# A fused four-block transformer kernel on one core: FFN weight splits moved to earlier places, and copies of the attention stage exchanged between two engines

## The reference, cut to what matters

```python
x = x + L0_xattn(layernorm(x), ctx, ctx)   # 16 heads, 4 kv heads, rotary, causal softmax, @ w_out.T
x = x + L0_ffn(layernorm(x))               # silu(gate) * up, width 1376, with shared and routed low-rank terms
x = x + L1_xattn(layernorm(x), ctx)        # sim = (x @ kv) @ kv.T, normalised over keys, softmax
x = x + L1_ffn(layernorm(x))               # 64 experts, 8 per token, width 192
```

## Time and profile before

| | |
|---|---|
| median of 3 runs | 1283.7 us (1283.13 to 1284.74) |
| profiled execution: time | 1284.93 us |
| profiled execution: span | 1283.1 us |
| mean granted clock of TensorE | 0.984 |
| PE busy | 1193.3 us (93%) |
| DVE busy | 723.9 us (56%) |
| ACT busy | 527.3 us (41%) |
| POOL busy | 483.4 us (38%) |

### The profile page before, as it was taken

One profiled execution on the slowest core, in us unless ns is written; L12 is line 12 of the kernel. 1 busy time (PEld: TensorE's weight loads), 2 busy tenths in 40 slices (PEclk: granted clock), 3 DMA queues, 4 the chain that ended last, 5 costly groups with the idle time before them and its releaser, 6 DMA issues.

```text
span 1283.1 us, 19538 instructions
## 1 busy us (share of the span) xinstructions
PE 1193.3 (93%) x6575; PEld 863.3 (67%) x6575; DVE 723.9 (56%) x1476; ACT 527.3 (41%) x1194; POOL 483.4 (38%) x541
## 2 busy tenths in 40 slices
PE   4899999999999999999999999999899999999990
PEld 3667777667777766777776687777456666666650
DVE  6966565686687678677868857554722222222220
ACT  4875221776412278542237853222333333333320
POOL 0440233462123446113353602121255555555530
PEclk8999999999999999999999999999999999999995
DMA  8012231002333000313300013632789999999847
GB/s 294 4 61 78 108 108 63 1 1 102 110 125 116 34 1 2 142 68 139 105 32 1 35 69 113 229 148 109 288 270 332 360 360 349 347 358 357 216 57 140
DMA packets 45906, 187.04 MB, mean 146 GB/s; under 512 B 6716, under 2 KB 9788, under 8 KB 31364
## 3 DMA queue, kind: packets, MB, share of 16 engines
q1 hardware_dynamic: 30964, 146.18, 30.2%
q0 software_dynamic: 14864, 39.85, 13.5%
HBM read 155.31 MB, written 34.90 MB: 148 GB/s over the span
## 4 chain that ended last, share of the span: by engine, by line
PE 73%; DVE 13%; ACT 5%; DMA 3%; issue 2%; POOL 2%; DVEq 0%; SPq 0%; POOLq 0%; ACTq 0%
PE PS L2568 14%; PE PS L1986 10%; PE PS L1988 10%; PE PS L1987 10%; PE PS L2584 4%; PE PS L2074 3%; PE PS L2588 3%; ACT P L892 3%; PE PS L2093 3%; DVE NM L1424 3%; PE PS L2558 2%; PE PS L2005 2%; DMA WRAW<-in_ffn 2%; PE PS L2385 1%; PE PS L2384 1%
## 5 line engine op out<-in xcount | busy, mean ns | idle before, releaser
L2568 PE MATMUL PS<-WE,XGT 128*128 128x384 f32 x512 | 192.7, 499 | 1.5 <-issue 1.5
L712 POOL CAST HH<-HID 128x512 fp32r<-128x512 f32 x44 | 37.3, 847 | 330.8 <-DVE HID L1792 330.8
L1019 ACT ACTIVATE WHI<-WRAW 128x1280 fp32r<-128x1280 f32 x44 | 56.0, 1273 | 226.5 <-DMA WRAW<-in_ffn 226.5
L1986 PE MATMUL PS<-XTH,WHI 128*128 128x512 f32 x352 | 141.1, 401 | 3.4 <-DVE WLO L1735 3.4
L1988 PE MATMUL PS<-XTH,WLO 128*128 128x512 f32 x352 | 138.2, 393 | 0.0
L1987 PE MATMUL PS<-XTL,WHI 128*128 128x512 f32 x352 | 137.9, 392 | 0.0
L892 ACT ACTIVATE P<-PS,NM 128x512 f32<-128x512 f32 (+3 forms) x256 | 131.9, 534 | 13.9 <-DVE NM L1424 12.9
L2568 PEld LDWEIGHTS PS<-WE,XGT 128*128 128x128 f32 x512 | 87.1, 190 | 56.7 <-issue 22.5
L1970 DVE COPY HMT<-PS 128x256 f32<-128x256 f32 x64 | 27.2, 425 | 163.8 <-PE PS L2577 159.3
L1424 DVE TENSOR_REDUCE NM<-PS 128x2 f32<-128x1024 f32 (+2 forms) x96 | 98.6, 1041 | 31.4 <-PE PS L1995 31.2
L2074 PE MATMUL PS<-ident,P 128*128 128x128 f32 x640 | 93.9, 278 | 14.8 <-ACT P L892 7.0
(11 more groups left out here) (341 smaller groups left out, 2733.1 us busy)
## 6 DMA issues: line engine op xcount, KB each, us to landing
WE<-in_we SPq DMA_DIRECT2D x64, 1152.0 KB
WRAW<-in_ffn SPq DMA_DIRECT2D x44, 1060.0 KB, 5.0
acc<-HN SPq DMA_DIRECT2D x17, 256.0 KB, 5.1
XIN<-in_x SPq DMA_DIRECT2D x4, 1024.0 KB, 6.4
out<-X SPq DMA_DIRECT2D x4, 1024.0 KB, 5.1
out<-acc POOLq DMA_DIRECT2D x1, 4096.0 KB, 23.0
hx<-HN SPq DMA_DIRECT2D x3, 1152.0 KB, 4.5
CTX<-in_ctx SPq DMA_DIRECT2D x4, 256.0 KB, 2.9
```

What stands on the lines that cost most here:

```text
L1019: act.activation(WHI[slot][:, 0:WD], WRAW[slot][:, 0:WD], ACT.Copy).then_inc(S["wg_hi"], 1)
L1986: pe.matmul(dst, a[0], b_[0], start=first, stop=False, **kw)
L2568: mm = pe.matmul(bank(2 + s % 2, 0, 2 * F1), XGT[s % 2][:, k, :], WE[s][:, k * 2 * F1:(k + 1) * 2 * F1], start=(k == 0), stop=(k == KC - 1))
```

## The change

It has four parts.

- **FFN weights.** The down half of chunk 0 and the gate and up half of chunk 1 are split on ACT between XN and the first XTH copies, and on DVE around the XTL operations; `wg_rest(0)` on DVE goes ahead of the first XTL. DVE's large operation of chunk 1 is cut in two, one part before XTL of row tile 3, one after; only its last operation stays behind LG. In chunk 1, `wg_hi(2)` and `wg_rest(2)` go ahead of SIL(1) and HID(1), and `wd_rest(1)` goes behind HID(1). The five clearing matmuls are taken out; the first product in each bank starts it.
- **Last group.** On DVE, the statistics of row tile 1 (`stats_x3(b, 1)`) go from before the maxima of units 4 and 5 to behind them.
- **Copies.** The copy of P(2, 0), the first of row tile 2, goes from DVE to ACT in group 2. In batch 0, and in group 2 of the others, stack 2 is copied by DVE and stack 3 by ACT, in place of the reverse. In group 1 with a tail, KST is copied before the maximum of unit 5. `exp_y(2)` goes further back on ACT.
- **Batch 0's projection.** Without a tail, row tile 2's products for k = 0 to 2 are made behind the last group's output, not ahead of it.

```diff
@@ turning_order
-            order += [("P", g, 2, 0, 1, "a" if g == G - 1 else "d"), ("P", g, 2, 1, 1, "a")]
+            order += [("P", g, 2, 0, 1, "a" if g > 1 else "d"), ("P", g, 2, 1, 1, "a")]
-                order += [("stack", g + 1, 2, "a"), ("stack", g + 1, 3, "d")]
+                order += [("stack", g + 1, 2, "a" if tail and g < 2 else "d"), ("stack", g + 1, 3, "d" if tail and g < 2 else "a")]
@@ scalar, attention
-                    if g == G - 1:
+                    if g > 1:
                         turned(g, 2, 0)
                     turned(g, 2, 1)
-                    if tail and g == 2:
-                        exp_y(2)
...
-                    if g < G - 1:
+                    if tail and g < 2:
                         stack(g + 1, 2, QST[1])
+                    elif g < G - 1:
+                        stack(g + 1, 3, QST[2])
                     if tail and g == 1:
                         exp_y(0)
+                    if tail and g == 2:
+                        exp_y(2)
@@ scalar, ffn
-                    if half == 1:
+                    if half == 0:
+                        act.wait_ge(S["dn_ps"], 1 + b * NF)
+                        wd_hi(0)
+                        wg_hi(1, 1, b * N1 + 1)
+                    else:
                         act.wait_ge(S["cov_ps"], 1 + b + 1)
...
-                    if not (isinstance(f, int) and f < 2):
-                        act.wait_ge(S["dn_ps"], 1 + b * NF + f - 1)
-                    wd_hi(slot)
-                    silu(f)
                     if f == 1:
                         act.wait_ge(S["up_ps"], 1 + b * NF + 1)
                         wg_hi(2, 0, next_loads)
-                wg_hi(1, 1, b * N1 + 1)
+                    if f > 1:
+                        act.wait_ge(S["dn_ps"], 1 + b * NF + f - 1)
+                    if f > 0:
+                        wd_hi(slot)
+                    silu(f)
@@ vector, attention
-                    if norm:
-                        n = stats_x3(b, 1)
                     if g > 0:
                         normalise(g - 1)
                     maximum(g, 4)
-                    if g < G - 1:
+                    if g < 2:
                         turned(g, 2, 0)
                     if sims:
                         similarity_scales(b)
                         y(0)
+                        stack(g + 1, 0, KST)
                     maximum(g, 5)
...
+                    if g < G - 1 and not (rows_in or sims):
+                        stack(g + 1, 2, QST[1])
...
-                    if norm:
-                        n = stats_x3(b, 2)
-                    if g < G - 1:
+                    if rows_in or sims:
                         stack(g + 1, 3, QST[2])
                     turned(g, 1, 0, 2)
+                    if norm:
+                        stats_x3(b, 1)
+                        n = stats_x3(b, 2)
@@ vector, ffn
+                wg_rest(0, 0)
                 turned_rest(0)
                 shifts(b, 2, 2, 4)
                 turned_rest(1)
-                wg_rest(0, 0)
+                dve.wait_ge(S["dn_ps"], 1 + b * NF)
+                wd_rest(0, 0)
+                wg_begin(1, 1)
                 turned_rest(2)
+                wg_part(1, 0, WB1 // 2)
                 turned_rest(3)
                 if b > 0:
                     dve.wait_ge(S["lgt_ps"], 1 + b)
                     gates_begin(b - 1, bank(1, 0, NT * E1).rearrange("p (t e) -> p t e", t=NT))
+                wg_low = wg_part(1, WB1 // 2, WB1)
...
-                    if not last and f > 1:
+                    if not last and f > 0:
                         wg_rest(f + 1, 1 - slot)
-                    wd_rest(f, slot)
+                    if f > 1:
+                        wd_rest(f, slot)
...
                     if f == 1:
-                        wg_rest(2, 0)
-                wg_rest(1, 1)
+                        wd_rest(1, 1)
+                step.need(wg_low)
+                wg_end(1, 1)
@@ tensor, attention
-                for t in range(NT - 1):
+                for t in range(NT - 1 if tail else 2):
...
-                    projected_out(t, KC - 1, KC).then_inc(S["op_ps"], 1)
+                    projected_out(t, KC - 1 if tail or t < 2 else 0, KC).then_inc(S["op_ps"], 1)
@@ tensor, ffn
-                            mm = pe.matmul(bank(4 + t), h[:, t * P:(t + 1) * P], part[:, WD:WD + C], start=False,
-                                           stop=False, skip_group_check=True)
+                            mm = pe.matmul(bank(4 + t), h[:, t * P:(t + 1) * P], part[:, WD:WD + C],
+                                           start=(h is HH[0] and part is hi), stop=False, skip_group_check=True)
...
-                    clear(4, 5)
...
-                clear(6, 7, 2)
```

More of the change, by code:

```diff
@@ L1022, in ffn, with wd_hi @@
                 wg_hi(0, 0, b * N0 + 1)
+                def wd_hi(slot):
+                    act.activation(WHI[slot][:, WD:WSPLIT], WRAW[slot][:, WD:WSPLIT], ACT.Copy).then_inc(S["wd_hi"], 1)
                 def normed(t):
@@ L1046, in ffn @@
                 act.activation(r8[0][:, :, :], projected[:, :, 0:E0], ACT.Exp, scale=-1.0).then_inc(S["sig_ready"], 1)
-                def wd_hi(slot):
-                    act.activation(WHI[slot][:, WD:WSPLIT], WRAW[slot][:, WD:WSPLIT], ACT.Copy).then_inc(S["wd_hi"], 1)
                 def silu(f):
@@ L1519, in attention @@
                         y(0)
+                        stack(g + 1, 0, KST)
                     maximum(g, 5)
                     if g < G - 1:
-                        stack(g + 1, 0, KST)
+                        if not sims:
+                            stack(g + 1, 0, KST)
                         if rows_in:
@@ L1728, in turned_rest, with wg_begin, wg_part, wg_end @@
                                           XTH[:, :, sl], ALU.subtract), "xT_lo", NT * b + t + 1)
-                def wg_rest(n, slot):
+                def wg_begin(n, slot):
                     dve.wait_ge(S["wg_hi"], 1 + b * NF + n + 1)
-                    step.post(dve.tensor_copy(WB2H[:, :], WRAW[slot][:, WB2:WCOLS]))
-                    step.need(step.post(dve.tensor_tensor(WLO[slot][:, 0:WB1], WRAW[slot][:, 0:WB1],
-                                                          WHI[slot][:, 0:WB1], ALU.subtract)))
+                    return step.post(dve.tensor_copy(WB2H[:, :], WRAW[slot][:, WB2:WCOLS]))
+                def wg_part(slot, c0, c1):
+                    return step.post(dve.tensor_tensor(WLO[slot][:, c0:c1], WRAW[slot][:, c0:c1], WHI[slot][:, c0:c1],
+                                                       ALU.subtract))
+                def wg_end(n, slot):
                     sig(dve.scalar_tensor_tensor(out=WLO[slot][:, WB1:WD], in0=WB2H[:, :], scalar=low_rows[:, 0:1],
@@ L1737, in wg_rest @@
                         "wg_lo", b * NF + n + 1)
+                def wg_rest(n, slot):
+                    wg_begin(n, slot)
+                    step.need(wg_part(slot, 0, WB1))
+                    wg_end(n, slot)
                 def wd_rest(n, slot):
@@ L2395, in gate_up @@
                     lora(f, slot, 1)
-                def clear(*banks):
-                    for bk in banks:
-                        pe.matmul(bank(bk), zrow[:, 0:P], zrow[:, :], start=True, stop=False, skip_group_check=True)
                 def down_first():
@@ L2411, in ranks_down @@
                         for part in w:
-                            pe.matmul(bank(2, parts=LR), part[:, WAD:WAD + LR], h[:, :], start=False, stop=False,
-                                      skip_group_check=True)
+                            pe.matmul(bank(2, parts=LR), part[:, WAD:WAD + LR], h[:, :],
+                                      start=(h is HH[0] and part is hi), stop=False, skip_group_check=True)
                     pe.wait_ge(S["wd_lo"], 1 + b * NF + 1)
```

## The result

The changed kernel takes 1274.26 us (median of five runs, 1273.20 to 1277.35) against 1283.7 for the kernel before (five runs too): ratio 0.993, 95% interval 0.9916 to 0.9944. Its profiled execution took 1274.26 with a span of 1272.4, where the kernel before had 1284.93 and 1283.1.

The account below looks back on a forecast made before the run. TensorE was taken as the bound, busy 93% of the span. Batches 1 to 3 gain 4.5 us, batch 0 -0.4, attention 2.65: 6.75 off the profiled 1284.93 gives 1278.2, as a median 1277.0; range 1272 to 1283.5.

Parts of the forecast that it names:

- Batch 0's projection: Batch 0, row tile 2's nine matmuls behind the last group: worth zero, at best 1.2 us gained, at worst 0.1 lost.
- the forecast's own case: At HID(1) in each FFN, PE stands 1.1 us, leaving 1.6 gained; 1275 to 1279 us, chance 0.37.
- the rival without a stall: FFNs: HID(1) isn't late, the operations don't meet or don't exclude; 11.2 us gained, 1272.5, chance 0.20.
- the start of batches 1 to 3: Splits ahead of XTH hide in ACT's 2.19 us pause before the XTH copies; 0.1 us lost per batch.
- batch 0's start: No ACT pause there, so the added splits delay XTH(0), XTL(0) and the projection: 2.0 us lost, bounds 1.6 and 2.4.
- Chunk 1: Low half of chunk 1's weights: PE's wait for WLO goes, 0.5 us gained per batch.
- clears: Five zero-matmuls dropped per FFN: 0.84 + 0.61 = 1.45 us of PE per batch.
- WLO first: Before HID(1), the large WLO runs ahead of HL: PE stands 1.1 us, 1.6 gained per FFN; a small favourite.
- HL first: Before HID(1), HL runs ahead of WLO: PE stands 2.3 us, 0.4 gained per FFN; 1281.7, chance 0.30.
- Chunk 2's wait: PE's wait for chunk 2's low half, hanging on a transfer, goes as the slot frees sooner: 0.6 us per batch.
- The rival on the slower side: Splits ahead of XTH delay the projection by 2.0 us in every batch, with HL first: 1287.5, chance 0.10.
- Attention: Attention of all batches: last group 1.8 us, group 2 0.45, group 1 0.3, batch 0 0.1; 2.65 gained in all.

Follow-up runs that it names:

- e3: The changed kernel with the vector engine's `wg_rest(2)` put behind HID(1); 1276.85 us.
- e2: The kernel before with only the clearing zero-matmuls taken out; 1287.32 us, ratio 1.0033.
- e4: The changed kernel with batch 0's weight splits moved out of its front, to among and behind later XTH and XTL operations; 1271.99 us.
- e6: The kernel before with the attention edits alone, batch 0's projection left as it was; 1279.12 us, ratio 0.9967.
- e10: The kernel before with one edit: both row statistics of the last group behind the maxima and their copies; 1281.73 us.
- e12: The changed kernel with batch 0's output projection put back as before; 1274.51 us.
- e7: e3 with GpSimd's KVT x gam moved behind HL(1); 1277.17 us, ratio 0.9954.
- e8: e7 and e4 together, on the changed kernel; 1277.11 us, ratio 0.9946.
- e5: e2 with five zero-matmuls put right ahead of chunk 2's wait for WLO; 1286.89 us, ratio 1.0019.
- e9: e2 with five full 128-row matmuls into free bank 3 right ahead of chunk 2's wait for WLO; 1283.5 us, ratio 0.9998.

## Why the prediction was right, and where its terms were off

The forecast was 1277.0 and its sum 6.75; the trace has 9.9. The measured 1274.26 lies in the range, but 0.7 below the 1275 to 1279 that I gave to the forecast's own case, and nearer to the 1272.5 of the rival without a stall than to 1277.0. That the forecast's case is the one that came is shown by the traces (four waits for HID, about 1.1 each in steps), not by the time. One small term had the wrong sign, the start of batches 1 to 3; one was mis-sized beyond its bounds, batch 0's start; the others lie 0.05 to 0.4 under what came.

- **Chunk 1, clears, chunk 2, HID(1).** In batch 1 the gains at these four places are 0.65, 0.81, -0.34 and 0.69 (forecast 0.5, 0.84, 0.61 - 1.1 = -0.49, 0.6). "WLO first" was the case that came, at its price: 1.11 for 1.1. That WLO and HL keep each other out held in all four FFNs; which of the two went first I had no row for, and took as a small favourite, so that part is luck. The third differs because I added the slower first matmul behind a stall (0.50 for 0.40, 0.11 in steps) to the waits and left it out at the clears: 348.77 starts a slow one too, so the second pair of clears was worth 0.72, not 0.61. Chunk 1 and chunk 2 were worth 0.15 and 0.09 more than I read from the steps. The price rested on an order decided by 0.01 us. No run had HL first, so its price of 2.3 stays an estimate; e3, with HID(1) ahead of both, shows only that PE's stall then comes back as WLO's.
- **Chunk 2's wait.** I said that it hangs on a transfer and would go. It went in the changed kernel, where WHI(2) no longer waits for one (the ACT row above). e2 shows how much it had weighed: with it in place, taking the clears out gives nothing. Had the change left the split of the down part where it was, the clears would have given nothing. The prediction added 1.45 and 0.6 as though they were independent.
- **Batch 0's start.** XTL(0) came 1.58 late, by XTH(0), which stood behind the two splits (bounds 1.6 and 2.4, taken 2.0). The vector engine's `wg_rest(0)` was done by 105.19, 0.08 ahead of XTL(0), because the small power operation did not break its run: POOL's ran 103.29 to 104.10 beside the large WLO at 103.46 to 104.68, which took its own 1.22. Both have two operands in SBUF and POOL's started first, so by what the prediction made of the earlier trace rows WLO should have been held; why this pair doesn't exclude each other stays open. And 0.43 came back: the kernel before waited for XTL in the same front, later, a row that I had not weighed:

```profile
111.94 0.36 PE L1986 MATMUL PS<-acH,XTH 128*128 128x216 f32 x1 [0.43 <-DVE XTL L1727]
```

  The rows of the changed kernel:

```profile
103.29 0.81 POOL L672 TENSOR_TENSOR sm<-sm,mhalf 128x2 f32<-128x2 f32 x1 [4.76 <-DVE sm L1349]
103.46 1.22 DVE L1744 TENSOR_TENSOR WLO<-WRAW,WHI 128x1024 fp32r<-128x1024 f32 x1
104.59 1.06 ACT L1037 ACTIVATE XTH<-PS 128x512 fp32r<-128x512 f32 x2
105.27 0.69 DVE L1736 TENSOR_TENSOR XTL<-PS,XTH 128x512 fp32r<-128x512 f32 x1
```

  So 1.58 - 0.43 = 1.15, measured 1.14: below both bounds, the mis-sized term of the sum. The delay itself, 1.58, is next to the prediction's lower bound of 1.6; e4, without it, starts chunk 0 1.43 sooner. The 0.43 goes in e4 and in e6 too, so it belongs to the attention edits and not to the splits.
- **Starts of batches 1 to 3.** 0.1 lost was forecast, 0.07 gained: the splits fit into ACT's pause, as argued from the earlier trace rows. The rival on the slower side died here.
- **Attention.** Group 3 gave 0.60 as forecast, e10 by itself 0.58 to 0.61. Group 2 gave 0.30 (forecast 0.15), group 1 0.14 (0.1).
- **Batch 0's projection** is nothing, as said (e12).
- **Clock.** The sum spoke of no clock at all. In the changed kernel's profiled execution 0.94 was lost to it in the last list's stage, so that without it the 1274.26 would have been some 1273.3.

## What to carry to other kernels

Ask of every filler on the bottleneck engine what comes next on its stream: in front of a wait that something else sets, taking it out gives nothing (e2: -0.09 us at that wait, and then the clock). When a producer is late, look first at whether it waits for its own buffer; the second buffer for HID, with the order that it allows, gave what the reorderings of e3, e7 and e8 could not. When a move makes two engines that keep each other out fall due together, work out both orders: here the starts were 0.01 apart, and by the prediction's estimate the other order costs 1.2 us more per FFN.

## What the runs showed of the hardware that I had not expected

TensorE's granted clock can fall to 1.2 GHz in the middle of a stream that is 93% busy. It did behind a wait of 1.81 (e2), behind one of 1.77 (e8), and behind five one-row zero-matmuls with a wait of 0.61 (e5), each time for about 3.4 us and at a cost of about 1.6 us; it didn't behind five full matmuls with a wait of 0.72 (e9), nor, in the profiled executions, behind waits of 0.85 and 1.47 (the changed kernel), 1.05 (e3), 1.37 (e7), 1.58 (e8, batch 2) or 1.63 (e12, batch 0). It falls in some executions and batches and not in others at the same wait: e2 had the same 1.7 to 1.8 in all four FFNs and one fall. The changed kernel shows one too, in the stage of the last list, where PE is half idle; so do e6, e8 and e12, and the other traces don't (columns as in e2's stretches):

```profile
904.00:907.00 3.00, 1.53 (x20) 0.64 (x18) 3.00 (x7) 3.00 (x10) 2.83 (x2) 1.00 0.62 236
907.00:908.00 1.00, 0.41 (x8) 0.29 (x8) 1.00 (x3) 1.00 (x5) 0.00 (x0) 1.00 1.01 367
908.00:911.00 3.00, 2.96 (x30) 1.86 (x31) 2.86 (x9) 1.14 (x2) 0.00 (x0) 0.53 0.41 155
```

The kernel before had 1.00 throughout that stage. The clock also differs at the start: in e5 and e6 it is at its upper level from some 21.5 us on, in the kernel before and the changed one it is still at the lower one between 27.6 and 30.8, and batch 0's attention is 0.83 and 1.25 shorter in those two than in the kernel before. What decides it between executions stays open; that it accounts for the spread of single runs (1273.2 to 1277.35) is likely and was not shown.
